# Attention stage begun inside the second normaliser stage, with the scatter tables zeroed in steps and the projection weights loaded ahead of the rest

## Chip, cores and metric

One core of a Trainium2 chip runs the kernel. The metric is the device time of one execution in microseconds (us); the profile adds the time of every instruction on TensorE (PE, with PEld for its weight loads), VectorE (DVE), ScalarE (ACT), GpSimd (POOL), and SyncE (SP), whose work here is to issue DMAs. A name that ends in q (SPq, POOLq) is an engine's sequencer.

## What is computed

6250 tokens of 512 features, and a graph of 106250 edges with 64 features each, sorted by destination.

```python
xn = layernorm(x)
summed = segment_sum(edge_attr, dst, 6250)              # and the count of edges per node
agg = summed / maximum(count, 1)
gnn = xn + relu(concat([xn, agg]) @ W1 + b1) @ W2 + b2
q, k, v = split(xn @ W_qkv.T + b_qkv); q, k = sigmoid(q), sigmoid(k)      # 8 heads of 64
i = sum_d(q * sum_t(k));  o = sum_d(k * sum_t(q))       # sum_t runs over all tokens
i_hat = sum_d(q * sum_t(k / o));  o_hat = sum_d(k * sum_t(q / i))
vw = v * softmax(o_hat, over tokens)
kv = einsum('bshd,bshe->bsde', k, vw)                   # per token, over the heads
r = einsum('bshd,bsde->bshe', q / i, kv) * sigmoid(i_hat)
x = x + gnn + (r @ W_out.T + b_out)
x = x + gate * (layernorm(x) @ We[best] + be[best])     # one expert of 16, chosen from the mean over tokens
```

## The kernel before

Tokens are handled in 13 blocks (12 of 512, `BT`, and one of 106). Six parts run one after another: constants; the four **front stages**, which share one program per engine (`front_stages`); then `gnn_stage`, which reads the edge sums, and `expert_stage`.

The front stages are **project** (`project_stage`: layer norm, q, k, v and the x half of the first graph layer, each product as three matmuls on split operands), **norms** (`norms_stage`: q and k are read back, k stays in SBUF in the tensor `kept`, 100 KB of each partition, and the sums i and o are inverted), **scale** (`scale_stage`: the sums i_hat and o_hat from q, read again, and `kept`; its last ten or so small steps on DVE, PE and ACT form the softmax over tokens and write `mix_sb`, a weight for every token and pair of heads) and **attend** (`attend_stage`: per block four steps `scores`, `neighbours`, `mixing`, then `output` with W_out). A stage ends for an engine with `before.over(engine)`: a wait for the end of the stage before on DVE (or the last store).

**Edge work** runs beside all four. It comes in 105 batches (`load`): 103 of 1024 edges, handled as 8 tiles of 128, then one of 6 tiles and one of 10 edges; 831 tiles in all. A batch is done in two "quads" of four tiles. For a quad DVE compares destinations (`select`, L204 to L218) and works out rows (`rows`, L252 and L256), PE sums edges of one destination (`sum_tile`, L230), ACT copies the sums to SBUF (`keep`, L240), and POOL issues one accumulating indirect DMA for each tile (`scatter`, L272) into one of five tables in HBM, `tile % TABLES`. Two additions in flight to one table could lose a sum, so a scatter waits for the one before it to the same table. The first scatter waits until all five tables are zero (`zeroed`). The buffers hold four batches (`SLOTS`): the first keep and the first rows of batch g wait until POOL has issued the fifth tile of batch g - 3 (`sums_free`, L276). How many batches fall to each block of a stage is written out by hand: `SHARE_A` (57 batches beside project, after batch 0), `SHARE_B` (9 beside norms), `SHARE_C` (4 beside scale: 67 to 70), `SHARE_D` (34 beside attend: 71 to 104, three in each of eleven blocks and one in the twelfth). `spread` places the quads of a block at the slots between its steps. Edge data is loaded three batches ahead (`load_ahead`, on SP).

**SP's order at the start** (L584 to L605): block 0 of x, edge batch 0, five tables zeroed (1.66 MB each), the q, k, v weights (two halves of 1.5 MB), edge batches 1 to 3, the v bias, W1 (two halves of 1 MB), block 1 of x. DVE and ACT split all four weight pieces before they do anything for block 0, so edge batch 1 and the third v product follow the second half of W1.

**The entry of attend**: SP waits for `before.over`, loads q and k of block 0, W_out and v of block 0, stores part 0 of `mix_sb` to HBM and reads it back in another layout (16 DMAs of 8 KB, `load_mix`), stores the rest, then loads q and k of block 1, the biases and x. DVE clears `mix[1]`, multiplies the first scores by mix (`neighbours(0, 0)`, L1464), splits W_out (L311), waits for the biases and adds them (L1521), and only then comes to the first quad of batch 71. The tensors of attend take the SBUF space that `kept` and `inverse` had.

Of the kernel before, what the change touches and what calls it, by code (L numbers as in the profile page):

```python
# [5 lines left out]
ALU = mybir.AluOpType  # L6
ACT = mybir.ActivationFunctionType
AX = mybir.AxisListType
F32 = mybir.dt.float32
# [4 lines left out]
P = 128  # L14
# [112 lines left out]
def quads_of(g):  # L127

    m = shape_of(g)[0]
    return [(j, min(4, m - j)) for j in range(0, m, 4)]  # L130


class Edges:
# [128 lines left out]
    def scatter(self, pool, g, k):  # L262
        m, rows = shape_of(g)
        for j in range(m):
            tile = g * BATCH + j if g <= WHOLE else WHOLE * BATCH + LEFT[0][0] + j
            t = tile % TABLES
# [3 lines left out]
            if tile >= TABLES:  # L270
                pool.wait_ge(self.c.scattered[t], tile // TABLES * 16)
# [6 lines left out]
    def finish_pool(self, pool):  # L278
        for t in range(TABLES):
            pool.wait_ge(self.c.scattered[t], 16 * len(range(t, WHOLE * BATCH + sum(m for m, rows in LEFT), TABLES)))  # L280
# [252 lines left out]
def project_stage(nc, c, edges):  # L533
# [3 lines left out]
    with ExitStack() as ctx:  # L537
# [36 lines left out]
        added, tables_zero = sem("added"), sem("tables_zero")  # L574
        zero_set, bias_v_in = sem("zero_set"), sem("bias_v_in")
        me.sems = norm.sems + weights.sems + [v_mm, v_bank_free, v_stored, out_mm, out_free, added, tables_zero, zero_set, bias_v_in] + out_stored

    OUTS = QK + JH

# [8 lines left out]
    def sp_program(sp):  # L588
# [6 lines left out]
        sp.wait_ge(zero_set, 1)  # L595
        for t in range(TABLES):
            sp.dma_start(c.table[t].rearrange("(p b a) c -> p b (a c)", p=P, b=5),
                         zero[:, :].unsqueeze(1).to_broadcast([P, 5, TROWS // P * ECOLS // 5])
                         ).then_inc(tables_zero, 16)
# [108 lines left out]
    def dve_program(dve):  # L708
        edges.begin_dve(dve)
        dve.memset(zero[:, :], 0.0).then_inc(zero_set, 1)  # L710
# [51 lines left out]
    def zeroed(pool):  # L762
        pool.wait_ge(tables_zero, 16 * TABLES)
# [35 lines left out]
def by_head(bank, r, ns):  # L799


    return bank[0:r, 0:ns * P].rearrange("p (s j m) -> p s j m", s=ns, j=CH)[:, :, :, 0:CH]


def norms_stage(nc, c, edges, before):
# [31 lines left out]
    def sp_program(sp):  # L837
        before.over(sp)

        def load(b):  # L840
# [6 lines left out]
            sp.dma_start(c.kept[:, :, block_at(b)], c.qk[DIM:2 * DIM, block_at(b)].rearrange("(o p) t -> p o t", p=P)  # L847
# [10 lines left out]
    def pe_program(pe):  # L858
# [3 lines left out]
        def sums(b):  # L862
# [3 lines left out]
            if b:  # L866
                pe.wait_ge(io_kept, b)
            head_sums(pe, c, io_bank, [q[b % U][:, j, 0:n] for j in range(CH)],
                      [c.kept[:, j, block_at(b)] for j in range(CH)], n).then_inc(io_mm, 1)
# [293 lines left out]
def attend_stage(nc, c, edges, before):  # L1163
# [67 lines left out]
    def sp_program(sp):  # L1231
# [39 lines left out]
        for i, (g0, g1) in enumerate(MIX_PARTS):  # L1271
# [6 lines left out]
            if i == 0:  # L1278
                load_mix(0)
# [1017 lines left out]
```

## Time and profile before

| | us |
|---|---|
| median of three runs | 2268.01 |
| the runs | 2262.24, 2268.39, 2268.01 |
| the profiled execution | 2260.96 |
| its span, first to last instruction | 2259.2 |

| stretch of the span | what runs |
|---|---|
| 0 to 69 | constants, start of project |
| 69 to 908 | project |
| 908 to 1073 | norms |
| 1073 to 1135 | scale |
| 1131 to 1694 | attend (its first load to the next part's first DMA) |
| 1694 to 2259 | graph layer, expert |

The profile gives busy times of each engine over the span, groups of like instructions, what each engine waited for, and a timeline. "Idle before" in brackets at a timeline row is the time for which that engine had done nothing, and after the arrow stands what released it; "issue" means that nothing in the profile shows what held it.

### The profile page before, as it was taken

To read this page: it belongs to the slowest core of one execution; us is meant where nothing else is said; L and a number is where in the kernel's file an instruction comes from. 1 tells how busy PE (TensorE), PEld (TensorE's weight loads), DVE (VectorE), ACT (ScalarE), POOL (GpSimd) and SP (SyncE) were. 2 spreads that over 40 slices of the span, in tenths; PEclk is the share of its full clock that TensorE was granted. 3 is DMA by queue.
4 is the path that set the end of the run, shared out by engine and by line. 5 is a ranking of instruction groups with operands and counts; after the bars stand their busy time and mean duration, and the time that the engine had idled before them with its cause. 6 is when DMAs were issued, how large, how long until landed. Compare 5 with 4: busy or idle time off the path is not lost. (4 is left out here: it accounts for less than half of the span.)

```text
span 2259.2 us, 31150 instructions
## 1 busy us (share of the span) xinstructions
PE 1923.5 (85%) x10775; PEld 1529.0 (68%) x10775; DVE 1221.2 (54%) x3855; ACT 560.9 (25%) x1314; POOL 1339.2 (59%) x876
## 2 busy tenths in 40 slices
PE   1899999999999999688728888786764999998598
PEld 1687887788888788344317777675653888886486
DVE  3544435434444432577436665555536888885575
ACT  2322232222232222111212212212112333333210
POOL 3688888888888888777638888878860000000100
PEclk9999999999999999765857878878886999999799
DMA  8677777787787777996997999999846666662784
GB/s 281 160 155 153 145 134 150 152 155 155 125 158 145 138 140 118 247 218 127 279 205 142 181 195 174 183 179 184 150 73 194 210 210 210 206 196 104 256 300 149
DMA packets 516664, 397.45 MB, mean 176 GB/s; under 512 B 348027, under 2 KB 385163, under 8 KB 516510
## 3 DMA queue, kind: packets, MB, share of 16 engines
q1 hardware_dynamic: 389870, 340.90, 53.3%
q0 software_dynamic: 126640, 54.59, 23.5%
q8 instruction: 85, 1.39, 0.2%
q14 instruction: 69, 0.57, 0.1%
HBM read 242.42 MB, written 152.96 MB: 175 GB/s over the span
## 5 line engine op out<-in xcount | busy, mean ns | idle before, releaser
L272 POOL DMA_INDIRECT table<-edge_sums,edge_row x831 | 1308.6, 1575 | 370.1 <-issue 292.3
L218 DVE SCALAR_TENSOR_TENSOR edge_sel<-edge_dst_all,edge_dst_f,upper 128x128 f32<-128x128 int16 x831 | 316.8, 437 | 106.1 <-PE edge_sum L230 80.4
L230 PEld LDWEIGHTS edge_sum<-edge_attr,edge_sel 128*128 128x128 f32 x1662 | 237.9, 215 | 139.9 <-DVE edge_sel L218 106.8
L324 PE MATMUL pr_out_bank<-pr_norm_xT_hi,pr_w_hi 128*128 128x512 f32 (+1 forms) x832 | 329.7, 396 | 0.0
L230 PE MATMUL edge_sum<-edge_attr,edge_sel 128*128 128x65 f32 x1662 | 252.6, 301 | 88.7 <-DVE edge_sel L218 83.9
L324 PE MATMUL pr_out_bank<-pr_norm_xT_lo,pr_w_hi 128*128 128x512 f32 (+1 forms) x832 | 320.7, 385 | 0.0
L324 PE MATMUL pr_out_bank<-pr_norm_xT_hi,pr_w_lo 128*128 128x512 f32 (+1 forms) x832 | 320.4, 385 | 0.0
L240 ACT ACTIVATE edge_sums<-edge_sum 128x260 f32<-128x260 f32 (+1 forms) x209 | 80.7, 386 | 628.6 <-PE edge_sum L230 472.4
L324 PEld LDWEIGHTS pr_out_bank<-pr_norm_xT_lo,pr_w_hi 128*128 128x128 f32 x832 | 156.6, 188 | 34.0
L324 PEld LDWEIGHTS pr_out_bank<-pr_norm_xT_hi,pr_w_lo 128*128 128x128 f32 x832 | 157.1, 189 | 29.7
L324 PEld LDWEIGHTS pr_out_bank<-pr_norm_xT_hi,pr_w_hi 128*128 128x128 f32 x832 | 157.0, 189 | 29.0
L324 PE MATMUL gn_acc<-gn_w_hi,gn_h_hi 128*128 128x512 f32 (+1 forms) x392 | 156.2, 399 | 6.3 <-DVE gn_h_lo L1886 6.3
L324 PE MATMUL gn_acc<-gn_w_lo,gn_h_hi 128*128 128x512 f32 (+1 forms) x392 | 156.7, 400 | 0.0
L324 PE MATMUL gn_acc<-gn_w_hi,gn_h_lo 128*128 128x512 f32 (+1 forms) x392 | 155.4, 396 | 0.0
L1977 POOL DMA_DIRECT2D x_rows<-gn_x x12 | 9.2, 764 | 245.7 <-DVE gn_x L1899 245.7
L732 DVE TENSOR_TENSOR pr_stage<-pr_v_bank,pr_bias_v 128x512 f32<-128x512 f32 (+1 forms) x49 | 33.9, 692 | 194.8 <-PE pr_v_bank L324 194.0
L1331 PE MATMUL at_s<-at_q,at_kt 64*128 64x128 f32 (+1 forms) x782 | 101.4, 407 | 29.8 <-ACT at_kt L1411 15.1
L691 ACT ACTIVATE pr_stage<-pr_out_bank,bias_qk 128x512 f32<-128x512 f32 (+1 forms) x104 | 68.8, 662 | 215.8 <-PE pr_out_bank L324 197.3
L694 ACT ACTIVATE pr_stage<-pr_out_bank 128x512 f32<-128x512 f32 (+1 forms) x104 | 59.5, 572 | 228.6 <-PE pr_out_bank L324 217.7
L324 PE MATMUL at_acc<-at_wo_hi,at_r_hi 128*128 128x512 f32 (+1 forms) x196 | 88.3, 450 | 26.8 <-DVE at_r_lo L1478 26.8
L1331 PEld LDWEIGHTS at_s<-at_q,at_kt 64*128 64x128 f32 (+1 forms) x782 | 81.3, 234 | 42.8 <-issue 24.4
L447 DVE TENSOR_TENSOR pr_norm_xT_lo<-pr_turn,pr_norm_xT_hi 128x512 fp32r<-128x512 f32 (+1 forms) x49 | 33.8, 690 | 136.5 <-ACT pr_norm_xT_hi L441 121.7
(202 smaller groups left out, 3247.0 us busy)
## 6 DMA issues: line engine op xcount, KB each, us to landing
edge_dst_all<-dst SPq DMA_DIRECT2D x103, 256.0 KB
edge_attr<-in_edge_attr SPq DMA_DIRECT2D x103, 256.0 KB
qk_T<-pr_stage SPq DMA_DIRECT2D x48, 512.0 KB
h_pre_T<-pr_stage SPq DMA_DIRECT2D x48, 512.0 KB
gn_pre<-h_pre_T SPq DMA_DIRECT2D x12, 2048.0 KB, 9.9
done<-qk_T SPq DMA_DIRECT2D x16, 1024.0 KB
table<-edge_sums,edge_row POOLq DMA_INDIRECT x831
pr_norm_x<-in_x SPq DMA_DIRECT2D x12, 1024.0 KB
```

Source lines behind the costliest of these rows:

```text
L218: op = dve.scalar_tensor_tensor(out=self.sel[q][0:rows, j, 0:rows], in0=self.dst_all[k][0:rows, t:t + m * (rows - 1) + 1:m], scalar=self.d ...
L230: mm = pe.matmul(self.p_sum[q][0:rows, j * ECOLS:(j + 1) * ECOLS], self.sel[q][0:rows, j, 0:rows], self.attr[k][0:rows, j0 + j, :], start= ...
L240: act.activation(self.sums[k][0:rows, j0:j0 + w, :], self.p_sum[q][0:rows, 0:w * ECOLS] .rearrange("p (w c) -> p w c", w=w), ACT.Copy).the ...
L272: pool.indirect_dma_start(self.c.table[t], bass.IndirectOffsetOnAxis(ap=self.row[k][0:rows, j:j + 1], axis=0), self.sums[k][0:rows, j, :], ...
L324: mm = pe.matmul(out, a, c, start=first and i == 0, stop=last and i == n - 1)
L447: dve.tensor_tensor(lo, bank, hi.bitcast(F32), ALU.subtract).then_inc(self.split[s % len(self.split)], 1)
L691: act.activation(pair[p % RING][:, e % 2, 0:n], out_bank[e % 2][:, 0:n], ACT.Sigmoid, bias=c.bias_qk[:, i:i + 1], accum_out=part[k][:, i:i ...
L694: act.activation(pair[p % RING][:, e % 2, 0:n], out_bank[e % 2][:, 0:n], ACT.Copy).then_inc(out_free, 1)
L732: dve.tensor_tensor(v[0:r, i, :], v_bank[i % 2][0:r, :], bias_v[0:r, :], ALU.add).then_inc(v_bank_free, 1)
L1331: mm = pe.matmul(s_bank[half][0:w * HEADS, j * P:j * P + w * HEADS], kt[u][rows, t:t + w, :].rearrange("d t h -> d (t h)"), q[b % 2][rows, ...
L1977: pool.dma_start(c.x1[bass.ds(b * BT, n), :].rearrange("(s p) d -> p s d", p=P), x1[b % 2][:, :, :]).then_inc(x1_stored[b % 2], 16)
```

## The change

Scatter tables: a tile of the first batch goes to table `tile % 2`, one of the second batch to `tile % 3`, later ones to `tile % 5`; each table has its own wait for being zero. SP's order at the start: x block 0, edge batch 0, **tables 0 and 1**, the q, k, v weights, x block 1, edge batch 1, v bias, table 2, edge batch 2, W1, tables 3 and 4, edge batch 3.

`kept` is laid out block by block, so that blocks 0 to 10 form one piece, free once the scale stage's eleventh head sum (`io_mm` at 11) is done. The tensors that attend needs first are placed in that piece. PE, ACT and SP no longer wait for the end of scale before they begin attend: SP waits for `io_mm` at 11 and then loads q, k, W_out and v of block 0 and both biases. Half of the 16 mix loads of block 0 are issued by ACT. The first four quads of attend (batches 71 and 72) are done before its first `neighbours`; block 0 keeps the other two. DVE clears `mix[1]` after the split of W_out.

```diff
+def table_of(tile):
+    return tile % (2 if tile < BATCH else 3 if tile < 2 * BATCH else TABLES)
+def uses_of(t, last):
+    return sum(table_of(tile) == t for tile in range(last))
...
-            if tile >= TABLES:
-                pool.wait_ge(self.c.scattered[t], tile // TABLES * 16)
+            if uses_of(t, tile):
+                pool.wait_ge(self.c.scattered[t], uses_of(t, tile) * 16)
+            else:
+                self.zeroed(pool, t)
...
+    ZERO_AT = (0, 0, 1, 2, 2)
...
-        sp.wait_ge(zero_set, 1)
-        for t in range(TABLES):
-            sp.dma_start(c.table[t].rearrange("(p b a) c -> p b (a c)", p=P, b=5),
...
+        sp.wait_ge(edges.ones_set, SLOTS + 1)
+        zero_table(sp, 0)
+        zero_table(sp, 1)
         weights.load(sp, 0, 2)
-        for g in range(1, EARLY + LEAD):
-            edges.load(sp, g, g % SLOTS)
+        norm.load(sp, 1, 1, BT)
+        edges.load(sp, 1, 1)
         sp.dma_start(bias_v[:, :], c.b_v.partition_broadcast(P)).then_inc(bias_v_in, 16)
+        zero_table(sp, 2)
+        edges.load(sp, 2, 2)
         weights.load(sp, 2, 4)
-        norm.load(sp, 1, 1, BT)
+        zero_table(sp, 3)
+        zero_table(sp, 4)
+        edges.load(sp, 3, 3)
...
+def kept_block(c, b):
+    n = min(BT, TOKENS - b * BT)
+    return c.kept[:, b * CH * BT:b * CH * BT + CH * n].rearrange("p (o t) -> p o t", o=CH)
...
+    def load_mix(b, eng, first, step=2):
...
+        for t, g in mix_loads(sizes[b])[first::step]:
...
+    EARLY_FREE = 11
+    FIRST = 4
+    def quads_at(b):
+        return spread(share.quads(b)[FIRST if b == 0 else 0:], 6)
...
-        before.over(sp)
+        sp.wait_ge(before.io_mm, EARLY_FREE)
         load_qk(0)
         weights.load(sp)
         load_v(0)
+        sp.dma_start(bias[:, :], c.b2.partition_broadcast(P)).then_inc(bias_in, 16)
+        sp.dma_start(bias_out[:, :], c.b_out.partition_broadcast(P)).then_inc(bias_in, 16)
...
             if i == 0:
-                load_mix(0)
+                load_mix(0, sp, 0)
+        before.over(sp)
         load_qk(1)
...
-        before.over(pe)
         scores(0, 0)
+        for quad in share.quads(0)[:FIRST]:
+            edges.sum_tile(pe, *quad)
...
-        before.over(act)
         by_token(0, 0)
         weights.split_hi(act)
         by_token(0, 1)
+        for quad in share.quads(0)[:2]:
+            edges.keep(act, *quad)
+        load_mix(0, act, 1)
+        for quad in share.quads(0)[2:FIRST]:
+            edges.keep(act, *quad)
...
         before.over(dve)
-        dve.memset(mix[1][:, :, :], 0.0).then_inc(mix_clear, 1)
+        for quad in share.quads(0)[:FIRST]:
+            edges.select(dve, *quad)
+            edges.rows(dve, *quad)
         neighbours(0, 0)
         weights.split_lo(dve)
+        dve.memset(mix[1][:, :, :], 0.0).then_inc(prepared, 1)
```

## Rows read from the trace of the kernel before

**Rows 1.** The profile's page: busy time of each engine, share of the span, instructions.

```profile
PE 1923.5 (85%) x10775; PEld 1529.0 (68%) x10775; DVE 1221.2 (54%) x3855; ACT 560.9 (25%) x1314; POOL 1339.2 (59%) x876
```

**Rows 2.** Stretches: length, busy time (instructions) by engine, granted clock, DMA share, GB/s.

```profile
72.40:924.20 851.80, 825.20 (x4174) 679.31 (x4172) 346.54 (x1526) 241.60 (x508) 712.08 (x456) 0.99 0.77 147
...
1149.30:1182.50 33.20, 5.17 (x46) 4.75 (x48) 9.06 (x27) 1.39 (x2) 0.00 (x0) 0.50 0.91 204
1182.50:1684.60 502.10, 412.60 (x3404) 348.03 (x3400) 285.25 (x950) 95.71 (x138) 413.81 (x263) 0.81 0.89 165
```

**Rows 3.** Timeline of POOL: start, duration, instruction, idle before.

```profile
932.75 1.54 POOL L272 DMA_INDIRECT table<-edge_sums,edge_row  x1 [8.54 <-DVE edge_row L256]
...
1086.95 1.54 POOL L272 DMA_INDIRECT table<-edge_sums,edge_row  x1 [11.45 <-issue]
...
1147.68 1.56 POOL L272 DMA_INDIRECT table<-edge_sums,edge_row  x1 [0.30 <-issue]
1182.56 1.54 POOL L272 DMA_INDIRECT table<-edge_sums,edge_row  x1 [33.31 <-issue]
```

**Rows 4.** Timeline of ACT in attend: first keeps of batches 76 and 79.

```profile
1248.48 0.39 ACT L240 ACTIVATE edge_sums<-edge_sum 128x260 f32<-128x260 f32 x1 [7.94 <-PE edge_sum L230]
...
1289.53 0.39 ACT L240 ACTIVATE edge_sums<-edge_sum 128x260 f32<-128x260 f32 x1 [8.61 <-issue]
```

**Rows 5.** Waits over the span: us in total, times, longest.

```profile
ACT edge_sums L240 <- POOLq L276: 40.9, 5, 11.0
```

**Rows 6.** The DMAs that zero the tables: issues (ns, first and last start), time to landing.

```profile
L597 SPq DMA_DIRECT2D table<-pr_zero x5: 657/2090/4742, 10.8 to 18.9; - x5
...
DMA to landing us min/median/max: 10.8/17.5/23.5
```

**Rows 7.** Timeline of POOL at the start.

```profile
42.77 1.79 POOL L272 DMA_INDIRECT table<-edge_sums,edge_row  x1 [36.88 <-DMA table<-pr_zero]
...
57.48 1.55 POOL L272 DMA_INDIRECT table<-edge_sums,edge_row  x1 [0.31 <-issue]
...
72.40 1.54 POOL L272 DMA_INDIRECT table<-edge_sums,edge_row  x1 [9.67 <-issue]
```

**Rows 8.** Timeline of ACT at the start: the splits of the weights.

```profile
49.60 2.76 ACT L306 ACTIVATE pr_w_hi<-pr_stage 128x3072 fp32r<-128x3072 f32 x1 [1.12 <-DMA pr_stage<-in_w_qkv]
60.35 1.91 ACT L306 ACTIVATE pr_w_hi<-pr_norm_early 128x2048 fp32r<-128x2048 f32 x1 [7.98 <-DMA pr_norm_early<-in_w]
63.21 1.91 ACT L306 ACTIVATE pr_w_hi<-pr_norm_early 128x2048 fp32r<-128x2048 f32 x1 [0.95 <-DMA pr_norm_early<-in_w]
```

**Rows 9.** Timeline of the entry of attend: PE, SP and DVE.

```profile
1117.26 1.04 PE L789 MATMUL sc_io_bank<-kept,heads 128*32 128x512 f32 x8
...
1130.79 0.63 SPq L1236 DMA_DIRECT2D at_q<-qk_T  x1
...
1135.76 3.47 DVE L1517 MEMSET at_mix<- 128x4096 f32 x1 [0.80 <-issue]
...
1152.08 6.35 SPq L1256 DMA_DIRECT2D mix<-mix_rows  x16
...
1160.55 1.29 DVE L1464 TENSOR_TENSOR at_near<-at_s,mix 128x512 f32<-128x512 f32 x2 [21.32 <-DMA mix<-mix_rows]
1161.76 2.28 DVE L311 TENSOR_TENSOR at_wo_lo<-at_x,at_wo_hi 128x2048 fp32r<-128x2048 f32 x1
...
1176.79 0.69 DVE L1521 TENSOR_TENSOR at_bias<-at_bias,at_rest 128x512 f32<-128x512 f32 x1 [12.75 <-DMA at_rest<-in_b_out]
...
1179.30 1.28 DVE L1464 TENSOR_TENSOR at_near<-at_s,mix 128x512 f32<-128x512 f32 x2
...
1206.78 1.29 DVE L1464 TENSOR_TENSOR at_near<-at_s,at_mix 128x512 f32<-128x512 f32 x2 [0.67 <-PE at_s L1331]
```

**Rows 10.** Timeline, the end of the front stages: the last scatter, the next part.

```profile
1683.22 1.35 POOL L272 DMA_INDIRECT table<-edge_sums,edge_row  x1 [0.30 <-issue]
...
1694.32 2.59 SPq L1693 DMA_DIRECT2D gn_agg_raw<-table  x5
```

More of the change, by code:

```diff
@@ L279, in finish_pool @@
         for t in range(TABLES):
-            pool.wait_ge(self.c.scattered[t], 16 * len(range(t, WHOLE * BATCH + sum(m for m, rows in LEFT), TABLES)))
+            pool.wait_ge(self.c.scattered[t], 16 * uses_of(t, WHOLE * BATCH + sum(m for m, rows in LEFT)))
     def scatter_all(self, pool):
@@ L573, in project_stage, with zero_table @@
         out_stored = [sem(f"out_stored{i}") for i in range(RING)]
-        added, tables_zero = sem("added"), sem("tables_zero")
-        zero_set, bias_v_in = sem("zero_set"), sem("bias_v_in")
-        me.sems = norm.sems + weights.sems + [v_mm, v_bank_free, v_stored, out_mm, out_free, added, tables_zero, zero_set, bias_v_in] + out_stored
+        added, tables_zero = sem("added"), [sem(f"tables_zero{i}") for i in range(3)]
+        bias_v_in = sem("bias_v_in")
+        me.sems = norm.sems + weights.sems + [v_mm, v_bank_free, v_stored, out_mm, out_free, added, bias_v_in] + tables_zero + out_stored
     OUTS = QK + JH
+    ZERO_AT = (0, 0, 1, 2, 2)
+    def zero_table(sp, t):
+        sp.dma_start(c.table[t].rearrange("(p b a) c -> p b (a c)", p=P, b=5),
+                     zero[:, :].unsqueeze(1).to_broadcast([P, 5, TROWS // P * ECOLS // 5])
+                     ).then_inc(tables_zero[ZERO_AT[t]], 16)
     def groups(n):
@@ L709, in dve_program @@
         edges.begin_dve(dve)
-        dve.memset(zero[:, :], 0.0).then_inc(zero_set, 1)
+        dve.memset(zero[:, :], 0.0).then_inc(edges.ones_set, 1)
         for g in range(EARLY):
@@ L868, in sums @@
             head_sums(pe, c, io_bank, [q[b % U][:, j, 0:n] for j in range(CH)],
-                      [c.kept[:, j, block_at(b)] for j in range(CH)], n).then_inc(io_mm, 1)
+                      [kept_block(c, b)[:, j, :] for j in range(CH)], n).then_inc(io_mm, 1)
         def turn(b):
@@ L1067, in sums @@
             head_sums(pe, c, io_bank[b % 2], [q[b % U][:, j, 0:n] for j in range(CH)],
-                      [c.kept[:, j, block_at(b)] for j in range(CH)], n).then_inc(io_mm, 1)
+                      [kept_block(c, b)[:, j, :] for j in range(CH)], n).then_inc(io_mm, 1)
         def turn(b):
@@ L1229, in mix_loads @@
         return [(t, len(range(t, n, GT))) for t in range(GT)]
+    def load_mix(b, eng, first, step=2):
+        part = [i for i, (g0, g1) in enumerate(MIX_PARTS) if g0 <= b * CH < g1][0]
+        eng.wait_ge(mix_stored[part], 16)
+        rows = c.mix[b * BT:b * BT + sizes[b], :]
+        for t, g in mix_loads(sizes[b])[first::step]:
+            src = rows[t:t + (g - 1) * GT + 1:GT, :].rearrange("g (a h) -> a g h", a=HEADS)
+            eng.dma_start(mix[b % 2][t * HEADS:(t + 1) * HEADS, 0:g, t * HEADS:(t + 1) * HEADS], src
+                          ).then_inc(mix_in[b % 2], 16)
+    EARLY_FREE = 11
+    FIRST = 4
+    def quads_at(b):
+        return spread(share.quads(b)[FIRST if b == 0 else 0:], 6)
     def sp_program(sp):
@@ L1248, in load_v @@
                 sp.dma_start(v[b % 2][0:left, full, :], rows[at:at + left, :]).then_inc(v_in[b % 2], 16)
-        def load_mix(b):
-            part = [i for i, (g0, g1) in enumerate(MIX_PARTS) if g0 <= b * CH < g1][0]
-            sp.wait_ge(mix_stored[part], 16)
-            rows = c.mix[b * BT:b * BT + sizes[b], :]
-            for t, g in mix_loads(sizes[b]):
-                src = rows[t:t + (g - 1) * GT + 1:GT, :].rearrange("g (a h) -> a g h", a=HEADS)
-                sp.dma_start(mix[b % 2][t * HEADS:(t + 1) * HEADS, 0:g, t * HEADS:(t + 1) * HEADS], src
-                             ).then_inc(mix_in[b % 2], 16)
         def load_x(b):
@@ L1608, in _ @@
             edges.begin_pool(pool)
-            project.zeroed(pool)
+            edges.zeroed = project.zeroed
             edges.scatter_all(pool)
```

51 lines of the change are left out of this document (26 added, 25 removed).

## The prediction, made before the changed kernel had run

> **What bounds the kernel now.** I read four views. The page first [rows 1]: PE is busy for 85% of the span and POOL for 59%, which points at PE, but these are averages over parts that have different limits. The busy times by stretch come next [rows 2]. Beside project, from 72.4 to 924.2, PE is busy for 825.2 of 851.8 us: PE sets that stretch. In 1182.5 to 1684.6, nearly all of attend, PE has only 412.6 of 502.1. POOL's 413.8 looks alike, but it comes from 263 scatters, so a scatter takes 502.1 / 263 = 1.909 us from start to start, and the timeline of POOL shows what lies between two of them: 0.30 us, each time [rows 3]. POOL has no other idle time there. This stretch is as long as its 263 scatters. That POOL holds back the others, and not they POOL, shows in how the work is made and in the waits. Batches 76 and 79, one block apart, have their first keep at 1248.48 and 1289.53 [rows 4]: ACT and PE make three batches in 41.05 us, while POOL needs 24 x 1.909 = 45.8 for them. The buffers fill, and then ACT waits for POOL, 40.9 us in five waits [rows 5].
>
> So up to 1684 the time is that of POOL's row of scatters, which can be shortened only where POOL stands still, and by starting it all sooner. The timeline of POOL shows the large gaps [rows 3]: 8.54 at 932.75 and 11.45 at 1086.95, at the entries of norms and scale, and 33.31 before 1182.56, at the entry of attend. From 1149.30 to 1182.50 POOL is at 0.00, PE at 5.17 and DVE at 9.06 of 33.20 us [rows 2]. The part after attend begins 11.1 us after the last scatter's start [rows 10] and is not touched.
>
> **The change, part by part.** Times in this part are on the clock of the trace of before, until the sum.
>
> *The gap at attend's entry.* In the trace DVE walks through a chain of loads there [rows 9]. SP's first load goes out at 1130.79. The mix store sits behind 4 MB of loads in the same queue and has landed by 1152.08, when the 16 mix loads go out; `neighbours(0, 0)` follows at 1160.55, the split of W_out at 1161.76, the bias addition only at 1176.79, after 12.75 us for a DMA. Only then, free at 1176.79 + 0.69 = 1177.5, does DVE select batch 71, whose first scatter is at 1182.56, 5.1 us later. In the changed kernel four quads come before all this, and need nothing from the chain. DVE is free at 1135.76, where the clearing of `mix[1]` stood [rows 9]; with the same 5.1 us the first sums are there at 1140.9. POOL's last scatter of batch 70 starts at 1147.68, so the next can start at 1149.5. The gap goes: 1182.56 - 1149.54 = **33.0 us**. Batches 71 and 72 last POOL 16 x 1.909 = 30.5 us, to 1180.
>
> *Does the gap come back later?* Batch 73 and those after it come from block 0 and the blocks behind it, so their time depends on the chain. SP starts when the eleventh head sum is done, at 1118.3 [rows 9], 12.5 us sooner. The mix store then lands at 1152.1 - 12.5 = 1139.6, plus 1.4 for two bias loads of 0.25 MB now ahead of it (by the 1 MB in 2.86 us below): 1141.0. The mix loads took 1160.55 - 1152.08 = 8.5 until DVE had them. Half of the issues move to ACT, which at best saves half of 6.35; I take nothing, since ACT comes to them after its splits and two keeps. The load is on the same path as before, SP's. By the Trainium skill (DMA: Bandwidth & Descriptors, Issuing engines are not separate DMA queues) issuing from two engines saves the sequencer's issue time only; taken so, it would be 3.2 us off the chain, and nothing off the sum below. So `neighbours(0, 0)` is at 1149.5, and behind it lie 1.2 for itself, 2.28 for the split, 3.47 for the clearing that was moved there, 0.7 for the bias sum, and 1.9 for the first quad of batch 73: `neighbours(0, 1)` at 1159.1 in place of 1179.30, 20.2 sooner. Batch 76 would have its first keep at 1248.5 - 20.2 = 1228.3, even with no credit for the four quads taken out of block 0; POOL comes to it 40 scatters after 1149.5, at 1225.9. That would be a gap of some 3 us. But four of block 0's six quads are gone from it, each at least the 1.9 us of DVE above, so the credit is likely more than 3. I take 1 us of new gap, and 0 and 12 as bounds (12: neither the bias pair's earlier place nor the credit helps, so that production is only 12.5 sooner). From there on production gains 45.8 - 41.0 = 4.8 us a block on POOL, as before, and the cover grows.
>
> What is queued behind the new waits: ACT waits for the mix store before its keeps of batch 72, until 1141 and then eight issues at 0.4 [rows 9], 1144 in all. POOL wants batch 72 at 1149.5 + 15.3 = 1164.8. Hidden; if the store came as late as before (1152.1) it would be hidden still. SP waits for `io_mm` with nothing behind it but attend's own loads. Loading W_out, q and k earlier adds 4.5 MB to the queue while scale finishes, but scale's last load is already ahead in the same queue: nothing. The new layout of `kept` keeps rows of 2 KB in HBM and of 512 elements for PE: nothing.
>
> *The start.* Project can run freely once DVE has split the second half of W1, whose landing releases ACT at 63.21 [rows 8]; the first quad of batch 1 and so the scatter at 72.40 follow it. Ahead of W1 in the one queue now stand five tables, the first landing at 10.8 + 10.8 = 21.6 and the last at 18.9 + 23.5 = 42.4 [rows 6], thus 5.2 each. Two of them move behind it: -10.4. From 49.60 to 60.35 [rows 8] three edge batches, the v bias and 1 MB of W1 landed; at 1 MB in 63.21 - 60.35 = 2.86, W1 took 2.9 and the bias 0.7, which leaves 2.4 for an edge batch. Batch 3 moves behind: -2.4. Block 1 of x, 1 MB, moves ahead: +2.9. Sum **-9.9 us**, bounds -7.5 (tables and edges by their bytes at 2.86 us a MB: 2 x 4.5 + 1.4 - 2.9) and -12.8 (x costs nothing, since the queue had room). Since PE fills the stretch after it [rows 2], all of project moves by this, and so do norms, scale and attend, because each waits for the one before. The q, k, v weights land before 49.60 by three tables, so PE's first two products are no limit.
>
> *Few tables.* POOL starts when two tables are zero: 21.6 + 5.2 = 26.8 in place of 42.77 [rows 7]. Alone this is worth nothing: batch 0 was issued by 62.7 and POOL then waited 9.67 us for batch 1 [rows 7]. The danger is the other way. The wait for the same table falls after 2 scatters (3.7 us) in batch 0, 3 (5.6) in batch 1. How long a scatter takes to land no row shows. The sixth scatter, at 57.48, waited for the first one's landing and shows no idle time beyond the 0.31 [rows 7]: at most 14.7 us, with the queues full; the nearest bound below is the 1.55 us of the issue. By the bound, batch 0 would end at 26.8 + 4 x 14.7 = 85.6 and batch 1 at 124.8, against 77.5 wanted (72.4 + 14.9 - 9.9): POOL 47 us behind. I take 5 us for a landing, nearer to the issue than to a bound that nothing reached: batch 0 ends at 47, before batch 1 is made, and nothing is lost. At 10 us batch 0 would end at 66.8 and batch 1 at 93.5, 16 behind, and this too costs nothing in the end: the gaps of 8.54 and 11.45 [rows 3] take it up. By the Trainium skill (DMA: Bandwidth & Descriptors, Anatomy of one DMA) such a transfer takes some 2.0 us plus its bytes at 436 GB/s; for 33 KB that would be 2.1 us and no hold-up at all. No row here shows it, and the sum would be the same.
>
> **The sum.** -33.0 + 1.0 - 9.9 = **-41.9 us**. The profiled execution took 2260.96, 7.05 under the median of 2268.01, and the three runs lie from 2262.24 to 2268.39. I take the middle, 2264.5: **2222.6 us**. A measurement of this kernel can tell about 0.3% from no change, 6.8 us.
>
> **Rivals.**
> *A, the gap comes back in part* (0.14). If production is only 12.5 us sooner the new gap is 12, or if an edge batch that attend needs lands behind its 5 MB of loads. Against it: data of 71 and 72 is loaded in scale. Gain 33 - 12 + 9.9 = 30.9: 2233.6.
> *B, the start does not move* (0.11). The order of the queue is not what holds W1, or PE loses it at block 0 to another late load. For it: SP's queue is full there, so issue times stall. Gain 32: 2232.5.
> *C, attend is bound by PE once POOL is early* (0.05). From the second block 41.05 x 11 us from 1179.1 (1159.1 + 20) reach 1631, and POOL ends at 1684.6 - 33 = 1652, so PE has 21 us in hand. Only a lower clock than the 0.81 of that stretch [rows 2] could use them up, below 0.81 x 41 / 45.8 = 0.73. At 0.70 a block takes 47.5 and the end is 20 later: 2243.
> *D, more than the sum* (0.05). x free and no new gap, and keeps of ACT less held: 2264.5 - 46 - 3 = 2215.
> *E, slower: the wait for the same table* (0.03). Its place is the first 16 scatters; its price is 8/2 + 8/3 = 6.7 landings against 29.7 us. It decides only when POOL is later than the 20 us of the two spare gaps and the 41.9 gained, thus from a landing of (77.5 + 61.9 - 26.8) / 6.7 = 17 us, above the 14.7 that the trace allows. At 20 us POOL is 83 us late: 2264.5 + 83 - 62 = 2286.
> The change does what it says in the forecast, chance 0.62.
>
> **Numbers.** The forecast's own range is 2264.5 - 46 to 2264.5 - 33, with 3 us on either side for the execution: 2215 to 2235. With A and B and half of C the range is 2212 to 2240, which leaves out 0.1 or so. Faster by over 0.3%: 0.94. Within: 0.03, where C is worse than its price or E near its point. Slower: 0.03.
>
> **What would show it right or wrong.** Right: ACT's split of the second half of W1 at about 53; POOL's first scatter at 27; the gap before batch 71 at 0.3 and its first scatter near 1140; no gap over 3 us until the last scatter near 1641; the entry gaps of norms and scale still there; the part after it 574 us as before. Wrong: POOL idle for DMA of the tables in the first 16 scatters; a gap of 10 or more behind batch 72 or 73; ACT no more waiting for POOL late in attend, which would be C.

## The result and the profile after

| us | before | after |
|---|---|---|
| median (runs) | 2267.26 (4) | 2231.89 (4) |
| lowest, highest | 2262.24, 2268.39 | 2230.45, 2234.79 |
| the profiled execution | 2260.96 | 2234.79 |
| its span | 2259.2 | 2233.1 |

The ratio is 0.985, with an interval of 0.9832 to 0.9868: 35 us faster. Predicted were 2222.6 us, from 2212 to 2240. The profiled execution of before took less than each of the four runs of the table, that of after was the slowest of its own, so the two traces differ by 26.2 us only.

Most marks that the prediction named can be read from a few rows. The page first, against [rows 1]:

```profile
PE 1920.9 (86%) x10775; PEld 1522.4 (68%) x10775; DVE 1222.2 (55%) x3855; ACT 560.4 (25%) x1314; POOL 1341.5 (60%) x876
```

The same instructions and the same work; what went is idle time. The timeline of POOL at the start (start, duration, instruction, idle before, what ended it), against [rows 7]:

```profile
29.16 1.79 POOL L286 DMA_INDIRECT table<-edge_sums,edge_row  x1 [23.28 <-DMA table<-pr_zero]
31.26 1.55 POOL L286 DMA_INDIRECT table<-edge_sums,edge_row  x1 [0.31 <-issue]
36.97 3.05 POOL L286 DMA_INDIRECT table<-edge_sums,edge_row  x1 [4.16 <-DMA table<-edge_sums,edge_row]
40.33 3.80 POOL L286 DMA_INDIRECT table<-edge_sums,edge_row  x1 [0.30 <-issue]
51.16 1.54 POOL L286 DMA_INDIRECT table<-edge_sums,edge_row  x1 [7.03 <-DMA table<-edge_sums,edge_row]
53.92 1.55 POOL L286 DMA_INDIRECT table<-edge_sums,edge_row  x1 [1.21 <-DMA table<-edge_sums,edge_row]
59.18 1.54 POOL L286 DMA_INDIRECT table<-edge_sums,edge_row  x1 [3.71 <-DMA table<-edge_sums,edge_row]
62.79 1.56 POOL L286 DMA_INDIRECT table<-edge_sums,edge_row  x1 [2.07 <-DMA table<-edge_sums,edge_row]
66.47 1.54 POOL L286 DMA_INDIRECT table<-edge_sums,edge_row  x1 [2.13 <-issue]
```

With two tables, each scatter waits for the one two before it: 36.97 - 29.16 = 7.8 us from one start to the next on the same table, and for the fifth to the eighth scatter 14.2, 13.6, 8.0 and 8.9. (The fourth did not wait: it went out 9.1 us after the second, behind the third.) Batch 0 ends at 64.4, just before batch 1 is made. ACT and SP there, against [rows 8]: the split of the second half of W1, and what SP issued before.

```profile
57.28 1.91 ACT L320 ACTIVATE pr_w_hi<-pr_norm_early 128x2048 fp32r<-128x2048 f32 x1 [0.80 <-DMA pr_norm_early<-in_w]
```
```profile
28.47 7.73 SPq L621 DMA_DIRECT2D pr_bias_v<-in_b_v  x1
...
40.74 3.82 SPq L315 DMA_DIRECT2D pr_norm_early<-in_w  x2
```

The second half of W1 is split 5.9 us sooner than before. SP stood 7.73 us in the issue of a small bias and came to W1 at 40.74. In the trace of before the same bias took 0.73 and W1 went out at 52.74, so W1 was issued 12.0 us sooner and landed only 5.9 sooner. POOL's row where it had its gaps [rows 3], and its end [rows 10]:

```profile
928.93 1.54 POOL L286 DMA_INDIRECT table<-edge_sums,edge_row  x1 [6.44 <-DVE edge_row L268]
...
1085.57 1.54 POOL L286 DMA_INDIRECT table<-edge_sums,edge_row  x1 [11.61 <-issue]
...
1148.23 1.54 POOL L286 DMA_INDIRECT table<-edge_sums,edge_row  x1 [0.31 <-issue]
1150.08 3.63 POOL L286 DMA_INDIRECT table<-edge_sums,edge_row  x1 [0.30 <-issue]
1154.01 4.50 POOL L286 DMA_INDIRECT table<-edge_sums,edge_row  x1 [0.30 <-issue]
...
1656.36 1.35 POOL L286 DMA_INDIRECT table<-edge_sums,edge_row  x1 [0.30 <-issue]
```
```profile
1666.57 2.58 SPq L1744 DMA_DIRECT2D gn_agg_raw<-table  x5
```

The 33.31 are gone: batch 71 follows batch 70 at once. But two of its scatters now take 3.63 and 4.50 us where others take 1.55. The trace of before has three such scatters as well, two at the start and one in batch 70. Its POOL and its DVE at these moments:

```profile
48.58 4.72 POOL L272 DMA_INDIRECT table<-edge_sums,edge_row  x1 [0.30 <-issue]
...
1132.08 4.17 POOL L272 DMA_INDIRECT table<-edge_sums,edge_row  x1 [0.30 <-issue]
```
```profile
48.51 3.36 DVE L311 TENSOR_TENSOR pr_w_lo<-pr_stage,pr_w_hi 128x3072 fp32r<-128x3072 f32 x1 [16.89 <-ACT pr_w_hi L306]
...
1131.40 3.56 DVE L1150 TENSOR_TENSOR done<-weight,gate 128x512 f32<-128x512 f32 x3
```

The first of them ends at 53.30, 1.43 us after the TENSOR_TENSOR beside it (51.87), the other at 1136.25, 1.29 after its own (1134.96). The part on f1 and f2 comes back to this. The chain of attend's entry, against [rows 9]:

```profile
1148.79 1.29 DVE L1512 TENSOR_TENSOR at_near<-at_s,mix 128x512 f32<-128x512 f32 x2 [6.62 <-DMA mix<-mix_rows]
1149.99 2.28 DVE L325 TENSOR_TENSOR at_wo_lo<-at_x,at_wo_hi 128x2048 fp32r<-128x2048 f32 x1
1153.08 3.47 DVE L1570 MEMSET at_mix<- 128x4096 f32 x1 [0.80 <-issue]
1156.47 0.63 DVE L1572 TENSOR_TENSOR at_bias<-at_bias,at_rest 128x512 f32<-128x512 f32 x1
...
1158.92 1.28 DVE L1512 TENSOR_TENSOR at_near<-at_s,mix 128x512 f32<-128x512 f32 x2
```

**Where the time went in the two profiled executions**, mark by mark, after less before: split of W1 -5.9, end of project -5.8 (902.8 for 908.6), end of norms -1.6 (1071.7 for 1073.3), batch 71 -34.3, last scatter -26.9, next part -27.8, end of the span -26.1. So four things took something back: norms lasted 168.9 for 164.7 us (4.2), batches 71 and 72 lasted 5.1 longer (35.1 from the first scatter of 71 to the first of 73, for 29.9 before), the 31 batches from there to the last scatter 2.3, and the part after attend 1.7.

### The profile page after: what moved, and what is told of

Read it like the earlier page. It is cut to its first block and busy times, and to the rows that moved or that the text cites. A ratio compares the mean times of both kernels' runs of the same rounds, so it can differ in the third digit from the quotient of the medians.

```text
span 2233.1 us, 31150 instructions
## 1 busy us (share of the span) xinstructions
PE 1920.9 (86%) x10775; PEld 1522.4 (68%) x10775; DVE 1222.2 (55%) x3855; ACT 560.4 (25%) x1314; POOL 1341.5 (60%) x876
## 5 line engine op out<-in xcount | busy, mean ns | idle before, releaser
L242 PEld LDWEIGHTS edge_sum<-edge_attr,edge_sel 128*128 128x128 f32 x1662 | 230.6, 210 | 131.8 <-DVE edge_sel L230 106.5
L242 PE MATMUL edge_sum<-edge_attr,edge_sel 128*128 128x65 f32 x1662 | 244.9, 296 | 80.0 <-DVE edge_sel L230 79.7
```

The costliest lines, as they stand in the source:

```text
L242: mm = pe.matmul(self.p_sum[q][0:rows, j * ECOLS:(j + 1) * ECOLS], self.sel[q][0:rows, j, 0:rows], self.attr[k][0:rows, j0 + j, :], start= ...
```

## The experiments

Twelve kernels ran; each was timed against the kernel before in five rounds. The marks that tell them apart, from their traces:

| | split of W1 | project ends | norms takes | batch 71, gap before it | last scatter | next part | ratio |
|---|---|---|---|---|---|---|---|
| before | 63.2 | 908.6 | 164.7 | 1182.6, 33.3 | 1683.2 | 1694.3 | |
| after | 57.3 | 902.8 | 168.9 | 1148.2, 0.3 | 1656.4 | 1666.6 | 0.985 |
| e1 start only | 56.6 | 902.5 | 168.8 | 1180.7, 33.2 | 1683.2 | 1693.4 | 0.9976 |
| e2 attend only | 63.0 | 907.8 | 165.1 | 1148.2, 0.3 | 1657.4 | 1665.2 | 0.9871 |
| e3 layout only | 63.9 | 909.2 | 165.4 | 1184.0, 33.0 | 1681.3 | 1690.5 | 1.0004 |
| e4 W1 first | 40.6 | 906.7 | 163.6 | 1146.6, 0.3 | 1654.8 | 1662.7 | 0.9849 |
| f1 no early quads | 56.0 | 901.8 | 165.6 | 1157.7, 14.5 | 1658.5 | 1669.3 | 0.9892 |
| f2 late loads | 55.7 | 901.6 | 165.4 | 1144.9, 2.0 | 1659.5 | 1671.3 | 0.9878 |
| f3 five tables | 55.6 | 902.0 | 168.5 | 1146.8, 0.3 | 1653.6 | 1665.1 | 0.9848 |
| f4 more in norms | 55.7 | 902.2 | 175.0 | 1121.8, 0.3 | 1626.6 | 1653.9 | 0.9832 |
| g1 same again | 55.1 | 900.8 | 164.3 | 1141.7, 0.3 | 1647.2 | 1655.6 | 0.985 |
| g2 balanced | 40.5 | 882.0 | 174.6 | 1117.0, 0.3 | 1631.1 | 1653.9 | 0.9784 |
| h1 tail | 55.3 | 901.5 | 175.1 | 1120.3, 0.3 | 1640.4 | 1662.4 | 0.9807 |
| h2 balanced, tail | 41.2 | 885.1 | 174.1 | 1118.0, 0.3 | 1627.4 | 1641.3 | 0.9744 |

### The parts alone: e1, e2, e3

e1 is before with the change's new tables and its order of loads; e2 is before with all of the rest (layout, early entry, early quads); e3 has of that only the layout. Its edit at the allocation (the loads and the readers of `kept` follow with `kept_block`):

```diff
-                nc.sbuf_tensor("kept", [P, CH, TOKENS], F32) as c.kept:
+                nc.sbuf_tensor("kept", [P, CH * TOKENS], F32) as c.kept:
```

> The kernel before with the new start alone (order of the loads, tables zeroed in steps, few tables for the first two batches); kept, scale and attend as before. Theory A, that norms takes the start's gain back through its own waits and not through the layout of kept: project ends 5.8 us sooner than before (its end at 902.8), norms ends only 1.5 sooner, and the ratio to before is 0.999 to 1.000. Theory B, that the new layout of kept costs norms 4 us: here the layout is the old one, so norms keeps its 164.7 us, all later parts come 5.8 sooner, POOL's gap before batch 71 stays 33, and the ratio is 0.9975.

> The kernel before with the early attend stage and the new layout alone; the start as before. Both theories: POOL's gap before batch 71 is 0.3 us, its scatters of batch 71 take some 5 us more than usual beside attend's first loads, and the last scatter starts near 1657. Theory A: norms takes the 164.7 us of before, the whole gain is some 26 to 30 us, ratio 0.987. Theory B: norms takes 169, the gain is 4 us less, ratio 0.989, last scatter near 1660.

> The kernel before with kept laid out block by block and nothing else. Theory A: nothing changes, norms 164.7 us, ratio 1.000. Theory B: norms takes 169 us, all after it comes 4 us later, ratio 1.0018.

Measured: ratios 0.9976 [0.9962, 0.9989], 0.9871 [0.9847, 0.9896] and 1.0004 [0.9989, 1.0019]. The layout costs nothing that these runs can tell, and norms keeps its 165 us in e2 and e3: theory B is out. The entry of attend carries most of the gain, 1.29% or 29 us; the start alone gives 0.24% or 5.4 us (2.5 to 8.6 by the interval), and the two add up to the 1.5% of the whole change. e1 fits neither theory as a whole: its trace has the marks of theory A (norms at 168.8, the last scatter where it was before), its median the ratio that was forecast for B. The trace of one execution and the median say different things about the start.

### W1 ahead of more: e4

```diff
-        weights.load(sp, 0, 2)
+        weights.load(sp, 0, 4)
...
-        weights.load(sp, 2, 4)
```

> The changed kernel with W1 loaded right behind the q, k, v weights, ahead of block 1 of x, edge batches 1 and 2, the v bias and table 2. Queue order theory (what lies ahead in the one queue sets when W1 lands): the second half of W1 lands near 45 in place of 57.3, the first quad of batch 1 then waits for its own data near 51, PE's steady work begins near 53 in place of 63.4, 10 us sooner. If project hands that on and norms takes back no more than 4 us, the ratio to before is 0.982, some 6 us below the changed kernel. Rival: SP's issue stalls set the landing, since the queue is full; then W1 lands no sooner than 52 and the ratio stays at 0.985.

Measured: 0.9849 [0.9813, 0.9885], as the changed kernel; the interval is wide, since one of six executions took 2211.08 us and the others 2230 to 2237, and it doesn't exclude the 0.982. The split of W1 came at 40.6, 16.7 us sooner than after the change: the theory of the queue's order holds, and the rival's 52 is out. ACT's keeps in project ran 23 us ahead of before up to batch 55. Then, in the timelines of ACT and of PE, and with PE alone by stretch (length, busy, instructions, granted clock, DMA share, GB/s):

```profile
850.69 0.39 ACT L252 ACTIVATE edge_sums<-edge_sum 128x260 f32<-128x260 f32 x1 [4.00 <-POOLq L290]
...
865.28 0.39 ACT L252 ACTIVATE edge_sums<-edge_sum 128x260 f32<-128x260 f32 x1 [7.69 <-POOLq L290]
```
```profile
866.05 0.45 PE L338 MATMUL pr_out_bank<-pr_norm_xT_hi,pr_w_hi 128*128 128x106 f32 x1 [2.77 <-ACT pr_stage L712]
```
```profile
840.00:855.00 15.00, 14.55 (x73) 1.00 0.75 125
855.00:870.00 15.00, 12.23 (x72) 0.86 0.66 110
870.00:885.00 15.00, 15.00 (x72) 0.50 0.41 41
885.00:900.00 15.00, 15.00 (x72) 0.50 0.40 32
```

The same stretches of the changed kernel:

```profile
870.00:885.00 15.00, 15.00 (x111) 1.00 0.79 126
885.00:900.00 15.00, 14.75 (x133) 1.00 0.59 58
```

ACT had to wait for POOL to free a buffer, PE stood still behind it for 2.77 us, and the granted clock fell from 1.00 (2.4 GHz) to 0.50 (1.2 GHz) and stayed there. PE was busy for all of 870 to 900, but with 144 instructions in place of 244. So project is bound by PE only as long as POOL follows: in the kernel before, POOL's 456 scatters of project, 712.08 us busy and 0.30 between two, need 849 of the 851.8 us of the stretch [rows 2]. I had read "PE sets project" and had not seen how near POOL is.

### Two parts of the new entry, and the few tables: f1, f2, f3

f1 leaves the four quads in block 0 (with `FIRST` at 0, ACT's keeps of these quads ahead of `neighbours` go too), f2 lets SP wait for the end of scale again, f3 goes back to `tile % 5` for all tiles, with the new order of loads:

```diff
-    FIRST = 4
+    FIRST = 0
...
-        for quad in share.quads(0)[:2]:
-            edges.keep(act, *quad)
         load_mix(0, act, 1)
-        for quad in share.quads(0)[2:FIRST]:
-            edges.keep(act, *quad)
```
```diff
-        sp.wait_ge(before.io_mm, EARLY_FREE)
+        before.over(sp)
```
```diff
-    return tile % (2 if tile < BATCH else 3 if tile < 2 * BATCH else TABLES)
+    return tile % TABLES
```

> The changed kernel, but with the four quads of batches 71 and 72 left in block 0 of attend (FIRST is 0); all loads stay early. Theory (the four quads close the gap): DVE comes to batch 71 only behind neighbours(0, 0), the split, the clearing and the bias addition, at about 1157.1, and its first scatter follows 5.1 us later, at 1162.2 in place of 1148.2; POOL shows one gap of about 14 before it, and near to the whole of that is in the time: ratio about 0.991 to the kernel before. Rival (the early loads alone close it, what is left is taken up by POOL's slower scatters): first scatter before 1155, ratio 0.985 to 0.987.

> The changed kernel, but SP waits for the end of scale before attend's first loads, as before the change; the four quads stay first. Theory (the chain of loads has to start early or the gap comes back later): batch 71 still follows batch 70 with a gap of 0.3; neighbours(0, 0) comes some 12 us later, at 1161; batch 76 would be kept at about 1238 where POOL wants it at 1226, so there are 8 to 14 us of new POOL gaps behind batches 72 to 76, and the ratio is about 0.990. Rival (the quads alone are the gain, the early loads give nothing that POOL's full buffers would not cover): no gap over 3 us, ratio 0.984 to 0.986. In either case the slow scatters, now 1150 to 1160, should move to where the loads are.

> The changed kernel and its new order of loads, but every tile goes to table tile % 5, so the fourth scatter waits until tables 3 and 4, now the last in the queue, are zero. Theory (few tables are only what lets the tables wait; POOL's lead in project is worth nothing, since PE's row sets project and the gaps at the entries of norms take POOL's delay): the fourth scatter at about 66, batch 1 begins at 76 to 78 in place of 66.5, POOL is some 10 us later through project, the gap of 6.4 before batch 58 falls to 0.3 and the one before batch 61 shrinks; from batch 64 on all is as in the changed kernel, ratio 0.985. Rival (POOL's row already is the bound beside project, so its start counts): all marks from batch 58 on are 8 to 10 us later, ratio 0.989.

Measured: 0.9892 [0.9868, 0.9915], 0.9878 [0.9857, 0.9898], 0.9848 [0.9827, 0.9868]. POOL in f1:

```profile
1157.72 1.54 POOL L286 DMA_INDIRECT table<-edge_sums,edge_row  x1 [14.48 <-issue]
```

and in f2:

```profile
1156.02 2.96 POOL L286 DMA_INDIRECT table<-edge_sums,edge_row  x1 [0.31 <-issue]
1159.28 4.52 POOL L286 DMA_INDIRECT table<-edge_sums,edge_row  x1 [0.30 <-issue]
...
1202.12 1.54 POOL L286 DMA_INDIRECT table<-edge_sums,edge_row  x1 [7.72 <-ACT edge_sums L252]
```

The gap of f1 is of the expected size. f2 has 7.7 and 2.0 us where 8 to 14 were expected, the 2.0 before batch 71, where none was; its ratio lies between the theory's 0.990 and the rival's 0.986. Against the changed kernel's ratio f1 costs 0.4% (9 us) and f2 0.3% (6 us), each known to 0.3% or so, so the cost of f2 is barely clear of noise.

That f1 loses less than its gap has a reason in the scatters: its batches 71 and 72 have none over 1.9 us and last 30.1 us, as before the change. Two things happen at the moment of the long pair, and both moved together in f1 and f2: SP starts its second group of loads (q of block 1), and DVE splits W_out, clears `mix[1]` and adds the biases. The times of the ends tell them apart (in us; four of the ten traces that have the pair):

| | SP's load starts | split of W_out ends | first long scatter ends | bias sum ends | second ends |
|---|---|---|---|---|---|
| after | 1151.46 | 1152.27 | 1153.71 | 1157.10 | 1158.51 |
| f2 | 1156.20 | 1157.56 | 1158.98 | 1162.38 | 1163.80 |
| g2 | 1135.99 | 1137.92 | 1139.36 | 1142.75 | 1144.16 |
| h2 | 1139.81 | 1141.00 | 1142.43 | 1145.82 | 1147.23 |

In all ten, the first long scatter ends 1.42 to 1.44 us after the split, and the second 1.41 to 1.43 after the bias sum; from the start of SP's load to the first end it is 2.25 to 3.37. So the pair goes with DVE. The three instances in the trace of before show the same, two of them at the start of the kernel and one 31 us ahead of this group of loads: every scatter of over 2.15 us in the fourteen traces, 65 in all, ends 1.28 to 1.44 us after a TENSOR_TENSOR of DVE that ran beside it. A clearing (MEMSET, 3.47 us) with nothing ready behind it does not do this: at 1135.76 before the change two scatters beside it took 1.56 and 1.54. In the changed kernel the bias sum stands right behind the clearing, and the scatter lasted until both were through. In f1 the split ran at 1145.54, within POOL's gap, and before the change at 1161.76, within the 33 us, where it cost nothing. No run alters DVE's part alone, and what holds POOL there is not shown.

In f3 the timeline of POOL says how little the early start was worth:

```profile
48.45 1.55 POOL L286 DMA_INDIRECT table<-edge_sums,edge_row  x1 [15.98 <-DMA table<-pr_zero]
66.51 1.55 POOL L286 DMA_INDIRECT table<-edge_sums,edge_row  x1 [16.52 <-DMA table<-pr_zero]
...
75.89 1.54 POOL L286 DMA_INDIRECT table<-edge_sums,edge_row  x1 [0.31 <-issue]
```

Batch 1 begins 9.4 us later than in the changed kernel, the gap of 6.44 before batch 58 is gone, and from batch 61 on all is within 1 or 2 us of the trace of after, and the ratio is the same: as the theory had it.

### The same kernel again: g1

> The changed kernel once more, not altered. It asks where the 4 us go that norms took longer in the first trace (168.9 in place of 164.7). Theory (the clock, which comes out differently from one execution to the next): project ends near 902, and norms takes either 165 with a granted clock of 0.7 or more between 902 and 950, or 169 with one near 0.62; length and clock go together in either case, and nothing else differs. Rival (an earlier start of norms costs it 4 us by its waits): norms takes 168.5 or more again, whatever the clock. Ratio 0.985 in both, within 0.002.

Measured: 2228.89 us, ratio 0.985 [0.9828, 0.9872]. The profiled execution was the fastest of its five, 2222.42 us with a span of 2220.7. PE between 902 and 950, in before, after, e1 and g1, in that order:

```profile
902.00:950.00 48.00, 30.54 (x170) 0.72 0.92 251
```
```profile
902.00:950.00 48.00, 31.25 (x143) 0.64 0.94 259
```
```profile
902.00:950.00 48.00, 32.39 (x143) 0.61 0.96 260
```
```profile
902.00:950.00 48.00, 33.26 (x165) 0.71 0.99 268
```

The first two have a granted clock of 0.72 and 0.64, and norms of 164.7 and 168.9 us. e1 has 0.61 and 168.8, g1 has 0.71 and 164.3, with the same program as after. The head sums of block 2, before, after and in g1, show where the time lies:

```profile
932.39 1.06 PE L789 MATMUL nm_io_bank<-nm_q,heads 128*32 128x512 f32 x8
```
```profile
928.62 1.93 PE L811 MATMUL nm_io_bank<-nm_q,heads 128*32 128x512 f32 x8
```
```profile
924.58 1.07 PE L811 MATMUL nm_io_bank<-nm_q,heads 128*32 128x512 f32 x8
```

Eight matmuls take 1.93 us at the lower clock and 1.06 at the higher. Length and clock go together, and the rival (168.5 us or more whatever the clock) is out. The 4 us are the clock's, not a wait of an earlier start: with the same nine batches and an earlier start norms took 164 to 166 in g1, f1, f2 and e4 (0.70 or 0.71), and 168 to 169 in after, e1 and f3 (0.61 to 0.64). What decides between the two in an execution is open; no run tells. (f4 and h1, with eleven batches in norms, were at 0.64.)

### Toward a better version: f4, g2, h1, h2

What was left of POOL's idle time in norms and at the entry of scale, 5.10, 6.89 and 11.61 us, asks for more edge batches there. f4:

```diff
-SHARE_B = [1, 1, 1, 0, 1, 1, 1, 0, 1, 1, 1, 0, 0]
+SHARE_B = [1, 1, 1, 1, 1, 1, 1, 0, 1, 1, 1, 1, 0]
...
-SHARE_D = [3, 3, 3, 3, 3, 3, 3, 3, 3, 3, 3, 1, 0]
+SHARE_D = [3, 3, 3, 3, 3, 3, 3, 3, 3, 3, 2, 0, 0]
```

g2 is e4 with `SHARE_B` of f4 and

```diff
-SHARE_A = [5, 4, 5, 4, 5, 5, 4, 5, 5, 4, 5, 5, 1]
+SHARE_A = [5, 4, 5, 4, 5, 5, 4, 5, 5, 4, 5, 4, 1]
...
+SHARE_D = [3, 3, 3, 3, 3, 3, 3, 3, 3, 3, 3, 0, 0]
```

h1 is f4, h2 is g2, with the batches of attend spread to its end:

```diff
+SHARE_D = [3, 3, 3, 3, 3, 3, 3, 3, 2, 2, 2, 2, 0]
```
```diff
+SHARE_D = [3, 3, 3, 3, 3, 3, 3, 3, 3, 2, 2, 2, 0]
```

> The changed kernel with 11 instead of 9 batches beside norms and 32 instead of 34 beside attend. Theory (POOL's row sets the end, and what is left to win is its idle time at 978, 1030 and 1086, 23.6 us less three times 0.3): the two batches fill these gaps, norms gets 4 to 8 us longer by their work on DVE and PE, but POOL is covered; last scatter about 22 us sooner than 1656.4, ratio 0.975 to 0.977. Rival (norms is the bound and what it grows by comes back): the gaps before batches 64 and 67 stay at 5 or more, or one of 8 to 10 comes at the entry of attend, ratio 0.981 or above.

> The changed kernel with W1 loaded ahead of block 1 and the later batches, as in e4, and 56, 11, 4 and 33 batches beside project, norms, scale and attend in place of 57, 9, 4 and 34. Theory (in e4 PE was 23 us ahead until it had to wait for POOL at the end of project, and then ran at a clock of 0.50; one batch less there keeps it from that wait): the clock stays at 1.00 until project ends, that is 885 to 890, and most of e4's lead reaches attend's end, which was the limit with 11 batches in norms; the next part begins at 1640 to 1645 in place of 1654, ratio 0.977 to 0.979. Rival (POOL's row is the limit whatever PE does; it begins only 3 us sooner and stands still for 10 to 20 us at the entry of norms, which now comes sooner): the last scatter is at 1640 or later, the next part 10.5 behind it, ratio 0.983 or above.

> f4 (11 batches in norms) with the 32 batches of attend placed as 3 in each of eight blocks and 2 in each of four, in place of 3 in ten and 2 in one. In f4 attend's own work ended 28 us behind the last scatter: its blocks went at POOL's pace of 45 us while they had three batches, and the last two blocks, without edge work, took another 57. Theory (edge work in the last blocks lets the ones before run at their own pace, so that attend's end and POOL's come together): last scatter as in f4, near 1627, the next part at 1638 to 1645 in place of 1654; ratio 0.977 to 0.979. Rival (attend is bound by its own work on PE and DVE): next part at 1652 or later, ratio 0.982 or above.

> g2 with its 33 batches of attend placed as 3 in each of nine blocks and 2 in each of three, in place of 3 in eleven. Theory, as for h1: last scatter near 1631, the next part some 11 us behind it, 1641 to 1646 in place of 1654; ratio 0.973 to 0.975. Rival: attend's own work, next part at 1652 or later, ratio 0.978.

Measured: f4 0.9832 [0.981, 0.9854], g2 0.9784 [0.9763, 0.9805], h1 0.9807 [0.9786, 0.9828], h2 0.9744 [0.9725, 0.9762]. f4 was a miss of a new kind. The last scatter came 29.7 us sooner than in the changed kernel, more than the 22 expected. But the next part begins 27.2 us behind it, where it had been 10.2:

```profile
1626.64 1.35 POOL L286 DMA_INDIRECT table<-edge_sums,edge_row  x1 [0.30 <-issue]
```
```profile
1653.85 2.69 SPq L1744 DMA_DIRECT2D gn_agg_raw<-table  x5
```

Attend's own work on PE and DVE now ends last: rival C of the prediction in its place, though not at its clock (0.81 from 1121.8 to 1653.9, where C wanted 0.73 or less). g2 met the ratio expected of it, but not by the expected marks: the next part begins at 1653.9, not 1640 to 1645. It keeps PE at full speed to the end of project and starts norms 20.2 us sooner than f4, but ends where f4 does. In g2 PE, by stretch:

```profile
860.00:870.00 10.00, 10.00 (x92) 1.00 0.66 89
870.00:880.00 10.00, 9.10 (x82) 1.00 0.50 52
```

Its clock is at 1.00 until project is done, which is the counterpart of e4's rows. With three batches in each of its first eleven blocks, attend goes at POOL's pace, and the blocks without edge work come after. h2 mends that, as expected, and the two ends come near each other:

```profile
1627.39 1.35 POOL L286 DMA_INDIRECT table<-edge_sums,edge_row  x1 [0.31 <-DMA table<-edge_sums,edge_row]
```
```profile
1641.33 2.73 SPq L1743 DMA_DIRECT2D gn_agg_raw<-table  x5
```

h2 is the fastest of all: 2206.47 us median (2202.4 to 2209.93). The same step does less in h1, where attend starts 18 us later: POOL waits 5.69 us before batch 103 and 4.39 before the last scatter, that of batch 104, both in the last blocks, and the last scatter moves from 1626.6 to 1640.4. The next part begins at 1662.4, where 1638 to 1645 were expected. By the marks my expectation for h1 was wrong; its ratio, 0.9807, can't be told from that of f4, and the profiled execution was the slowest of its five. That the edge work in the last blocks comes too late for POOL is my reading of the two waits.

## Why the prediction was right, and where not

- **What bounds the kernel.** Right for attend: POOL's row. It did have more idle time there than I wrote, 8.4 us in gaps of up to 2.29 beside the 0.30 between scatters; the 1.909 contains it. And standing still is not all that costs, as batches 71 and 72 show. For project it was incomplete (e4): PE's row and POOL's are equally long, which the change didn't touch but the next one would.
- **The gap at the entry, -33.0.** Right: 33.31 became 0.31, and e2 alone gives 0.9871. The chain was right as well: `neighbours(0, 0)` forecast at 1149.5 and `neighbours(0, 1)` at 1159.1 on the old clock, seen at 1148.79 and 1158.92; with all marks up to there some 1.4 us sooner, that is 1150.2 and 1160.3 on the old clock. New gap: 1 forecast; none over 0.9 us seen in the trace of after before batch 79. f2 shows that the early loads earn that: without them 7.72 before batch 74.
- **Batches 71 and 72 "last POOL 16 x 1.909 = 30.5 us".** This term failed: 35.1. I used the mean of a stretch for scatters that would now stand beside DVE's split of W_out and its bias sum; both had run while POOL was idle. The two long scatters give 3.63 + 4.50 - 2 x 1.56 = 5.0 us. The trace of before had the price: 4.72, 3.57 and 4.17 us for scatters beside such a TENSOR_TENSOR, at 48.58, 53.60 and 1132.08. I had moved DVE's work without asking what POOL does meanwhile, and put it at nothing.
- **The start, -9.9.** Right in sign, too large: the split of W1 moved by -5.9 in after and -8.1 in g1, and the timed gain of e1 is 5.4 us (2.5 to 8.6). What took the other 2 to 4 us is not shown. The order in the queue is the right cause (e4), but my prices by the item are off: by them e4's step was worth 2.9 + 2 x 2.4 + 0.7 + 5.2 = 13.6 us, and it gave 16.7 against after and 14.5 against g1. SP's issues took long there (7.73 for a bias), but don't explain it: W1 went out 12.0 us sooner and landed 5.9 sooner. Rival B (no gain at the start) is out by e1's ratio; and in the trace of g1, -8.1 at W1 is -7.8 at the end of project and -8.2 at the end of norms.
- **"All of project, and so do norms, scale and attend" move by it.** True in g1, not in the first trace of after, where norms gave back 4.2 by its clock. It is an execution's luck, but three of the seven profiled with an early start and nine batches in norms had it.
- **Few tables, landing 5 us.** Mis-sized: 7.8 to 14.2 from start to start while the first loads run, near the bound of 14.7; 1.5 to 3.8 of each is POOL's own issue. The Trainium skill (DMA: Bandwidth & Descriptors, Anatomy of one DMA) gives a fixed cost of about 2.0 us plus the bytes, by which I had an estimate of 2.1. The measured times do not agree with it beside the first loads, and they decide. My own sign of being wrong came, too: POOL was idle for DMA of the tables in the first 16 scatters, 7.03 us the longest. The conclusion stood, since batch 0 was issued at 64.4 and batch 1 was made only at 66.47, and f3 shows that the early start was worth nothing.
- **Rival C** was priced wrong by its own terms. With 21 us in hand over 11 blocks, a block may take 43.0 us, that is a clock of 0.77, not 0.73; at 0.70 the end would be 50 us later, not 20. It did not come: ACT still waited for POOL late in attend, 25.4 us in three waits.
- **The other signs.** Forecast were the split of W1 at about 53, batch 71 near 1140 and the last scatter near 1641. Seen were 57.3, 1148.2 and 1656.4 in after, 55.1, 1141.7 and 1647.2 in g1. The entry gaps of norms and scale are still there.
- **The sum.** Forecast -41.9. In the trace of g1: -8.1 for the start, -33.0 for the gap, +5.1 for batches 71 and 72, and the last scatter at -36.0; the next part follows at -38.7, the span at -38.5. In the trace of after 2.2 of this are missing at the start, 4.6 in norms and 2.6 in the rest of attend. The medians differ by 35, and g1's median is 33 under that of before, so the trace of g1 is a fortunate execution: it shows what the mechanism gives when the clock in norms comes out high.

## What to carry to other kernels

Before work is moved into a gap, ask what else runs in that gap, on every engine: here DVE's split had cost nothing only because POOL stood still. The price stood in the trace of before at another place, as three scatters of more than twice the usual length. When two engines' rows are nearly equally long, quickening one only fills the buffers, and the halt can cost the clock on top; balance how the other's work is shared out in the same step (h2 against e4). Compare a term of a few us in more than one execution, since a clock that comes out otherwise looks like a wait.

## What the runs showed of the hardware

- A scatter that POOL began beside one of DVE's TENSOR_TENSORs on SBUF tensors (the splits of the weights, the softmax weights, the bias sum) lasted until 1.28 to 1.44 us after that instruction's end, where others take 1.55 us: 65 scatters of 2.2 to 4.7 us in fourteen traces. Ten traces have a pair of them in attend (2.2 to 3.6 us, then 4.5); the other four have none there, since POOL was idle at that moment. A MEMSET with nothing ready behind it left the scatters beside it at 1.54 and 1.56.
- A wait of 2.77 us of PE inside project was followed by more than 30 us at a granted clock of 0.50, with PE busy all the time.
- The same program had a granted clock of 0.64 in one execution and 0.71 in another over the same 48 us, and 4.6 us of difference in norms.
- One DMA issue on SP can last 7.73 us (a bias of 512 numbers, at 28.47 after the change); the same issue took 0.73 at 51.97 before it. The DMA share was 1.00 or more around both.
